# A 16-layer selective scan and experts on one core: the residual kept with tokens on partitions, two more product tiles on GpSimd, new order of all lists

## The reference, cut to what matters

```python
h = rmsnorm(x, nw)
u, z = jnp.split(jnp.einsum('blh,ch->blc', h, in_w), 2, axis=-1)
u = silu(causal_conv(u, cw, cb))
proj = jnp.einsum('bli,ci->blc', u, xp_w)
dt_r, Bm, Cm = (proj[..., :R], proj[..., R:R + N], proj[..., R + N:])
dt = jax.nn.softplus(jnp.einsum('blr,ir->bli', dt_r, dtw) + dtb)
# selective_scan, one token after the other, state h of (I, N):
dA = jnp.exp(dt_t[:, :, None] * A)
h = dA * h + (dt_t * u_t)[:, :, None] * B_t[:, None, :]
y = jnp.einsum('bin,bn->bi', h, C_t)
...
y = (selective_scan(u, dt, A, Bm, Cm, dp) + u * dp) * silu(z)
return x + jnp.einsum('bli,hi->blh', y, ow)
```

## Time and profile before

| | |
|---|---|
| time, median of 3 runs | 13544.95 us (13542.22 to 13551.38) |
| the profiled execution | 13536.48 us, its span 13534.6 us |
| busy share: DVE, POOL, PE, ACT | 94%, 91%, 90%, 82% |
| instructions: DVE, POOL, PE, ACT | 7474, 4049, 51470, 21539 |
| DMA, mean over the span | 155 GB/s |

### The profile page before, as it was taken

The page is one execution under the profiler, slowest core; times in us unless marked ns, Lnnn a source line. Parts: engine busy times, 40 slices in busy tenths (PEclk is TensorE's granted clock), DMA queues, the critical chain, the costliest instruction groups (busy, mean ns, idle before and its releaser), DMA issues. The chain is left out here.

```text
span 13534.6 us, 194387 instructions
## 1 busy us (share of the span) xinstructions
PE 12204.6 (90%) x51470; PEld 6290.1 (46%) x51470; DVE 12710.1 (94%) x7474; ACT 11039.6 (82%) x21539; POOL 12315.3 (91%) x4049
## 2 busy tenths in 40 slices
PE   7999999999999999999999989999999999998899
PEld 4444444444444444444444444444444444444766
DVE  2999999999999999999999999999999999999543
ACT  4888888888888888888888888888888888888211
POOL 2999999999999999999999999999999999998033
PEclk8999999999999999999999999999999999999899
DMA  4555555555555555555555555555555555555122
GB/s 109 160 165 163 163 170 164 167 159 167 160 165 163 162 170 163 169 159 166 161 165 162 162 169 164 170 159 165 162 164 163 162 169 165 170 159 159 42 65 65
DMA packets 790401, 2092.82 MB, mean 155 GB/s; under 512 B 97428, under 2 KB 379988, under 8 KB 788176
## 3 DMA queue, kind: packets, MB, share of 16 engines
q1 hardware_dynamic: 693936, 1687.84, 36.3%
q0 software_dynamic: 95664, 403.36, 15.1%
q10 hardware_dynamic: 720, 0.55, 0.0%
HBM read 1418.92 MB, written 287.73 MB: 126 GB/s over the span
## 5 line engine op out<-in xcount | busy, mean ns | idle before, releaser
L1000 POOL TENSOR_TENSOR dbu<-dtu_rep,b_rep 128x1944 f32<-128x1944 f32 x2053 | 8984.0, 4388 | 163.6 <-DVE h L924 154.3
L924 DVE TENSOR_TENSOR_SCAN h<-ps,dbu 128x972 f32<-128x972 f32 x4103 | 8695.4, 2169 | 77.4 <-ACT ps L709 76.3
L709 ACT ACTIVATE ps<-dt_rep,A_cur 128x323 f32<-128x323 f32 x12312 | 5868.3, 522 | 1072.1 <-DVE h L924 1017.8
L530 PE MATMUL ps<-h,fold 128*32 128x486 f32 x16392 | 3743.2, 577 | 298.5 <-DVE y_gated L941 298.5
L932 DVE TENSOR_TENSOR h<-h,ps 128x1944 f32<-128x1944 f32 (+2 forms) x2050 | 3542.2, 1739 | 2.3 <-PE ps L517 2.3
L1009 POOL TENSOR_TENSOR h<-h,c_rep 128x972 f32<-128x972 f32 (+1 forms) x769 | 1953.9, 2541 | 0.0
L530 PEld LDWEIGHTS ps<-h,fold 128*32 128x32 f32 x16392 | 798.9, 109 | 2268.2 <-issue 2040.6
L600 PE MATMUL ps<-u_raw,w_cv 128*128 128x162 f32 (+7 forms) x8256 | 1800.5, 371 | 2.6 <-ACT terms L752 1.3
L600 PEld LDWEIGHTS ps<-u_raw,w_cv 128*128 128x128 f32 x8256 | 1359.0, 190 | 546.7 <-issue 206.0
L562 PE MATMUL ps<-x_norm,w_z 96*128 96x324 f32 (+1 forms) x4128 | 990.9, 384 | 145.9 <-ACT rstd L777 124.3
L587 PE MATMUL ps<-x_norm,w_u 96*128 96x324 f32 (+1 forms) x4128 | 991.3, 384 | 49.2 <-issue 45.2
(11 more groups left out here) (186 smaller groups left out, 11606.8 us busy)
## 6 DMA issues: line engine op xcount, KB each, us to landing
dtu_rep<-dtu_rows SPq DMA_DIRECT2D x1028, 486.0 KB, 4.7
dt_rep<-dt_rows SPq DMA_DIRECT2D x1028, 486.0 KB, 5.9
sums<-terms POOLq DMA_DIRECT2D x258, 972.0 KB, 6.7
b_rep<-b_rows SPq DMA_DIRECT2D x1028, 162.0 KB, 4.1
sums<-sums POOLq DMA_DIRECT2D x257, 486.0 KB, 4.5
dt_rows<-sums SPq DMA_DIRECT2D x257, 486.0 KB, 2.8
dtu_rows<-terms SPq DMA_DIRECT2D x257, 486.0 KB, 3.1
c_rep<-b_rows SPq DMA_DIRECT2D x770, 162.0 KB, 5.0
```

Source lines behind the costliest of these rows:

```text
L530: mm = pe.matmul(y_ps[32 * r:32 * r + 32, half, :], fold[:, :], flat(h, step)[:, half * YW:(half + 1) * YW], start=(s < NR), stop=(s == la ...
L709: ins = act.activation(decay[s % 2][:, it * L + 1:(it + 1) * L], dt_rep[:, s % NR, it, 1:L], ACT.Exp, scale=A_cur[:, it * N + s:it * N + s ...
L924: dve.tensor_tensor_scan(flat(h, s), decay[s % 2], flat(dbu, s), 0.0, ALU.mult, ALU.add).then_inc(s_scan, 1)
L1000: pool.tensor_tensor(steps(dbu, s, 2), steps(dtu_rep, r, 2), each(b_rep[:, q, :], 2), ALU.mult).then_inc(s_dbu, 1)
```

## The change

Five things change together.

1. In the layers and behind them the residual `x_R` has tokens on partitions (108 x 3 blocks x 192 channels for each sequence). The output product (`te_out`) therefore takes the gated y as the stationary operand and w_o as the moving one, and the gate (`ve_gate`) writes over z_act. `first_norm` ends with TensorE transposes of the normed residual and ScalarE copies into `x_R`.
2. The norm of a unit: ScalarE squares and adds up along the free dimension (`accum_out`), scales the three blocks by the reciprocal root, TensorE transposes (`te_turn`), and ScalarE writes x_norm with the norm's weight. The product with ones and POOL's x_norm product are gone, and so is the copy of the C rows, since xp_rows now has two buffers.
3. POOL makes product 12 whole (steps 12 and 13, 1944 columns); DVE has no part in it.
4. The ring of dbu has six slots instead of four (`DRING`, `FORMER`).
5. All five lists have a new order.

```diff
-DRING = 4
+DRING = 6
+FORMER = {0: 12 - N, 2: 14 - N, 4: 10 - N}
-PRODUCTS = (0, 2, 4, 6, 8, 10, 12, 14)
+PRODUCTS = (0, 2, 4, 6, 10, 8, 14)
 POOL_PRODUCTS = (3, 7, 12)
-SHARED = {12: 4}
+SHARED = {}
...
+                pe.wait_ge(s_log, B)
+                for b in range(B):
...
+                                mm = pe.transpose(turned(b, part)[:, c * H + half * HC:c * H + (half + 1) * HC],
+                                                  x_T[:, half, at:at + TS], cst["ident"][0:HC, 0:HC])
...
+                        act.copy(x_R[:, b * ROW + first * H:b * ROW + (first + n) * H], turned(b, part)).then_inc(s_kept, 1)
...
+        def te_out(pe, u, par, part, freed):
...
+            pe.matmul(pj[0:TS, 0:n * H], ident[0:TS, 0:TS], of_unit(u, first, n), start=True, stop=False)
...
+                    mm = pe.matmul(pj[0:TS, at:at + H], z_act[par][:, it, chunk(c)], w_o[:, it, :],
+                                   start=False, stop=(c == first + n - 1 and it == IT - 1))
...
+        def te_turn(pe, j, half, freed):
...
+                mm = pe.transpose(pj[0:HC, chunk(c)], scaled[:, c, half * HC:(half + 1) * HC], ident[0:TS, 0:TS])
...
-        def te_ss(pe, j, freed):
...
+                ins = act.activation(scaled[:, c, :], of_unit(j, c, 1), ACT.Square, accum_out=total[:, c:c + 1])
...
+        def se_scaled(act, j):
...
+                ins = act.activation(scaled[:, c, :], of_unit(j, c, 1), ACT.Copy, scale=rstd[:, c:c + 1])
...
+            act.activation(x_norm[par][:, half, :], pj[0:HC, 0:L], ACT.Copy, scale=nw_cur[:, half:half + 1]).then_inc(s_xn, 1)
...
-        ge_x_norm = x_norm_on
...
+            dve.tensor_tensor(z, y_ps, z, ALU.mult).then_inc(s_gate, 1)
...
-                ge_x_norm(pool, v[3], q[3])
...
+                ge_dtu(pool, v[2], q[2])
...
+                sp_store_dtu(sp, v[2])
```

More of the change, by code:

```diff
@@ L33 @@
 YW = IT * L // 2
+ROW = L // 108 * H
+OUTS = ((0, 2), (2, 1))
 NR = 4
 RING = 8
-DRING = 4
+DRING = 6
 EPS = 1e-5
@@ L78, in reached, with landed @@
         eng.wait_ge(s, count + BIAS)
+def landed(eng, s, count):
+    if not isinstance(count, int) or count > 0:
+        eng.wait_ge(s, 16 * count + 16)
 def raise_counts(eng, *sems):
@@ L274, in _ @@
                             mean(b)
+                pe.wait_ge(s_log, B)
+                for b in range(B):
+                    pe.wait_ge(s_out, b + 1)
+                    wait(pe, s_kept, 2 * (b - NG) + 2)
+                    for part, (first, n) in enumerate(OUTS):
+                        for c in range(n):
+                            at = b * L + (first + c) * TS
+                            for half in range(2):
+                                mm = pe.transpose(turned(b, part)[:, c * H + half * HC:c * H + (half + 1) * HC],
+                                                  x_T[:, half, at:at + TS], cst["ident"][0:HC, 0:HC])
+                        mm.then_inc(s_turn, 1)
             @block.vector
@@ L324, in _ @@
                             root((g - 1) * NG + i)
+                for b in range(B):
+                    for part, (first, n) in enumerate(OUTS):
+                        act.wait_ge(s_turn, 2 * b + part + 1)
+                        act.copy(x_R[:, b * ROW + first * H:b * ROW + (first + n) * H], turned(b, part)).then_inc(s_kept, 1)
 MAIN_SET = "natural_log_exp_and_others"
@@ L801, in se_dt @@
                 wait(act, s_fin, 16 * p)
-                wait(act, s_dst[0], 16 * p)
+                landed(act, s_dst[0], p)
                 reached(act, s_dtu, p)
@@ L1004, in ge_product @@
             at = POOL_PRODUCTS.index(s)
-            wait(pool, s_cr[at], 16 * (u + 1))
+            landed(pool, s_cr[at], u + 1)
             n = width(s)
@@ L1082, in sp_load_c @@
             sp.sem_inc(s_go, 1)
-            wait(sp, s_bst, 16 * (v + 1))
+            landed(sp, s_bst, v + 1)
             n = N + s // NR * 4
@@ L1092, in sp_store_dt @@
             for s in s_dtr:
-                wait(sp, s, 16 * v)
+                landed(sp, s, v)
             sp.dma_start(dt_rows, dt[:, :]).then_inc(s_dst[0], 16)
@@ L1100, in sp_store_dtu @@
             for s in s_dur:
-                wait(sp, s, 16 * v)
+                landed(sp, s, v)
             sp.dma_start(dtu_rows, dtu[:, :]).then_inc(s_dst[1], 16)
         def sp_load_dt(sp, v, r):
-            reached(sp, s_exp, turn(EXPS, v - 1, 12 + r))
+            reached(sp, s_exp, turn(EXPS, v - 1, last(EXPS, range(r, N, NR))))
             sp.sem_inc(s_go, 1)
-            wait(sp, s_dst[0], 16 * (v + 1))
+            landed(sp, s_dst[0], v + 1)
             sp.dma_start(dt_rep[:, r, :, :].rearrange("p i t -> p (i t)"),
@@ L1111, in sp_load_dtu @@
         def sp_load_dtu(sp, v, r):
-            reached(sp, s_dbu, turn(INPUTS, v - 1, (12 + r) // 2 * 2))
+            reached(sp, s_dbu, turn(INPUTS, v - 1, last(INPUTS, range(r // 2 * 2, N, NR))))
             sp.sem_inc(s_go, 1)
-            wait(sp, s_dst[1], 16 * (v + 1))
+            landed(sp, s_dst[1], v + 1)
             sp.dma_start(dtu_rep[:, r, :, :].rearrange("p i t -> p (i t)"),
@@ L1454, in exp_gate @@
                     act.activation(score_tiles(b), logits(b), ACT.Exp, scale=-1.0).then_inc(s_ge, 1)
-                for b in range(GS):
-                    square_x(b)
                 for g in range(N_G + 1):
-                    now, last, more = g < N_G, g > 0, g + 1 < N_G
+                    now, last = g < N_G, g > 0
+                    if now:
+                        for i in range(GS):
+                            square_x(GS * g + i)
                     act.preload_act_table_set(LOG_SET)
@@ L1467, in _ @@
                     act.preload_act_table_set(MAIN_SET)
+                    if last:
+                        for i in range(GS):
+                            root_n(GS * (g - 1) + i)
                     if now:
```

531 lines of the change are left out of this document (268 added, 263 removed).

## The result

The changed kernel takes 14861.32 us (median of 4 runs, 14854.63 to 14862.83) against 13543.58 for the kernel before beside it: ratio 1.0975, 95% interval 1.0962 to 1.0988. The forecast was 14890.

What follows compares the result with a forecast made beforehand. DVE was taken to bound the layers (47.58 us a pass), POOL close second; 46.85 + 2.15 + 3.6 = 52.6 a pass, so 13536.5 + 1285 + 35 + 31 = 14888, forecast 14890 us; likeliest case 14640 to 15180, 8 in 10 13850 to 15500.

Steps and rivals of the forecast that it cites:

- POOL's and DVE's work: Own work per layer pass without new waits: DVE 47.58 - 0.73, POOL 47.00 + 1.37 - 1.52, both 46.85 us.
- The first wait: POOL's sums<-sums waits for the accumulating DMA sums<-terms to land: 2.15 us a pass, bounds 1.57 and 2.38.
- the cover in the sum: POOL time between sums<-terms and sums<-sums: 0.87 us of issue plus one dbu, 5.13 us, against 7.3 start to start.
- The second wait: POOL's dbu 2 waits for dtu loads queued behind other loads: 18.6 - 15.0 = 3.6 us a pass, bounds 0 and 4.4.
- a w_cv reload: 768 KB load ahead of the last dtu load, once per layer: 2.3 us each, 16 times, +35 us.
- The two waits add: Both sit in POOL's order, so a pass takes 46.85 + 2.15 + 3.6 = 52.6 us, 5.02 more than before.
- its case of no wait: Rival, chance 0.10: transfers on POOL's queue and the dtu loads land in time; DVE and POOL tie at 46.85, 13380 us.
- The granted clock stays 1.00: Sign of being right: TensorE's granted clock in the layers stays at its full level, 1.00.
- more than both: Rival, chance 0.15: TensorE partly at half clock makes projection and convolution late, 2.1 us a pass on top, 15425 us.
- Two signs that were to show that the order binds elsewhere: Signs of being wrong: DVE waits for ScalarE's decays, and dt loads come late to ScalarE; no size given.
- Small terms: Once per run: residual transposes before the layers 31 us (bounds 13 and 60), final norm 0 within 20.
- the price by activations: ScalarE gets ten activations for six removed, at 0.52 us each 5.2 us gross, covered by its 5.8 us slack.

Runs made afterwards that it cites:

- both edits: Changed kernel with SyncE loading dtu blocks 2 and 3 earlier, and POOL issuing sums<-terms one product earlier (ScalarE's lost ahead of its second x_norm): 13930.78 us, 1.0294 of before.

## Why the prediction was right, step by step

- *POOL's and DVE's work.* Forecast 46.85 for both. POOL's is 46.8 by its waits in the changed kernel, and 49.0 less the 2.2 that it waits in the run with both edits. DVE did not come down as far: it is busy 2705.36 / 57.1 = 47.4 us a pass in the changed kernel and 47.2 with both edits, 0.2 to 0.3 less than before in place of 0.73. No run shows why. In the changed kernel it did not bind, since DVE waited 5.0 us a pass there.
- *The first wait.* Forecast 2.15 (start to start 7.3, cover 5.13, which is 2.17); measured 2.03, with 7.30 in the pass shown. In that pass 5.23 us stand between. That this came so near to the cover in the sum is partly luck: the issue takes 0.61 us to the next start, where the sum has 0.87, and the dbu 4.62 to its end, where the sum has 4.26 from its start to the next one. The wait was made by itself in the kernel before (1.96), and removed by itself. By the estimate of 4.28 us from DMA: Bandwidth & Descriptors in the Trainium skill (Anatomy of one DMA — SWDGE (gpsimd) path) neither kernel would have waited; the runs disagree, with 6.7 or 6.8 us to landing in each of them.
- *The second wait.* Forecast 3.6, and 2.3 more in the 16 passes with a w_cv reload, 3.74 in the mean; measured 3.50. That the means are so near is partly luck as well. In the stretch the six longest waits make up 36.4 of the 199.6 us, and the other 51 passes wait 3.2 us each in the mean, 0.4 less than forecast: in the pass shown dbu 2 came 6024.69 - 6006.67 = 18.0 us after dtu's end, against 18.55 in the sum, and POOL worked for 15.3 of them, against 15.0. Of the six, three have the w_cv reload and waited 5.39 to 5.65, some 2.3 more than the others, as priced. The other three (6.38 to 6.72) are the first pass of a layer: SP issues its next load 6.2 to 6.7 us after the first two of dtu, where it is 1.7 in the pass shown. The prediction has no term for these, and what holds SP there no run shows. Three loads moved gave about 3.0 us per 1000 KB. That the dtu loads queue behind other loads was shown twice, by all the loads in another order and by these three; that it is not SP's issue rests on these three alone (2.1 us of issue moved, less came back).
- *The two waits add.* In the changed kernel, yes. Removing them one at a time gave 3.23 and 1.32 us a pass. Removing both gave 3.64, not 4.55, because a third limit at about 49 us lay below, which the prediction did not look for: its case of no wait (46.85 a pass, 13380 us) was reached by none of the edits.
- *TensorE, and the signs of being wrong.* "The granted clock stays 1.00" was wrong: 0.90 in the stretch, 0.50 after the pauses in the passes read. The case "more than both" had the half clock right and its price wrong: the output came late, and 1.07 us of that was shown to lie in the time that POOL waited anyway. Two signs that were to show that the order binds elsewhere were there too: DVE waited 1.79 us a pass for decays, and ScalarE 23.5 / 57.1 = 0.41 for dt loads. They did not bind in the changed kernel: POOL's work and its waits make up the whole pass, and 0.8 us less of the waits for decays left it as it was.
- *Small terms.* The first gate came 25 us later, against 31 for the transposes; the end is 16 longer, against 0 within 20. Neither was looked at further. Two slips in the sum (2.15 for 2.17, and 35 for 16 times 2.3) are 7 us together.

## What to carry over

When an order by hand is changed, price what stands between a transfer and the instruction that waits for it, link by link, before counting the work removed: 0.73 us of DVE work that was to go was paid for with 5.7 us of waits, and the cover alone, in the old kernel, cost 3.6%. Count loads on one queue by their bytes ahead, and put those first that the pacing engine asks for first. And when two waits are removed together, expect less than their sum, and look for a loop through several engines that both waits may have belonged to, even where no engine is full; here such a loop was only argued.

## What was not expected of the hardware

In the two passes of the changed kernel that were read, TensorE ran for 10 to 13 us at the granted clock 0.50, after pauses of 2.84 and 4.16 us. With both edits it ran at 0.53 and 0.62 from 6040 to 6044, after pauses of 0.95 and 1.42 us. In the kernel before, with pauses up to 1.40 us, the clock stayed 1.00. What decides it, no run here separates. And an activation that accumulates carries a second row: the group by line of the squares has 174 activations of 352 ns and 174 reads of the accumulator of 187 ns, which the price by activations left out (three of each a pass; no run here shows that they cost time).

```profile
L810 ACT ACTIVATE scaled<-x_R 108x192 f32 x174 | 61.1, 352 | 0.0
...
L810 ACT ACTIVATION_READ_ACCUMULATOR scaled<-x_R 108x1 f32 x174 | 32.5, 187 | 0.0
```
